# A perceiver block on one core: the low parts of the next tile's query products for the last four heads on GpSimd instead of VectorE

## The reference

```python
q = layernorm(x) @ Wq;  k = ctx @ Wk;  v = ctx @ Wv        # split into 16 heads of 64
scores = einsum('bhsd,bhkd->bhsk', q, k) / 8
x = x + einsum('bhsk,bhkd->bhsd', softmax(scores), v).reshape(B, S, 1024) @ Wo + bo
x = x + self_attention(layernorm(x));  x = x + quantised_ffn(layernorm(x))
```

## Time and profile before

| | |
|---|---|
| median of the runs | 1576.76 us (1576.45 to 1576.85) |
| the profiled execution | 1575.99 us, span 1574.2 us |
| busy: TensorE, its weight loads | 1536.0 us (98%), 1282.0 us (81%) |
| busy: VectorE, ScalarE, GpSimd | 1058.1 us (67%), 737.9 us (47%), 371.2 us (24%) |
| low parts on VectorE, line 1086 | 62 of 1749 ns, 107.2 us |
| low parts on GpSimd, line 1314 | 2 of 3499 ns |
| cross attention by tiles | from about 188 to 1005 us of the span |
| granted TensorE clock | 0.996 |

### The profile page before, as it was taken

The page is one execution under the profiler, slowest core; times in us unless marked ns, Lnnn a source line. Parts: engine busy times, 40 slices in busy tenths (PEclk is TensorE's granted clock), DMA queues, the critical chain, the costliest instruction groups (busy, mean ns, idle before and its releaser), DMA issues.

```text
span 1574.2 us, 35899 instructions
## 1 busy us (share of the span) xinstructions
PE 1536.0 (98%) x13706; PEld 1282.0 (81%) x13714; DVE 1058.1 (67%) x2295; ACT 737.9 (47%) x1596; POOL 371.2 (24%) x225
## 2 busy tenths in 40 slices
PE   7999999999999999999999999999999999998989
PEld 5778788888998899989988898888878888786544
DVE  7666677677667766676677667647555654556788
ACT  5444655555545554555455554433222232224755
POOL 1000235343444344444434343500000000000000
PEclk9999999999999999999999999999999999999999
DMA  6899873341434233332333133250220311225022
GB/s 234 318 365 360 316 252 128 138 149 49 140 132 144 61 122 138 138 92 91 138 138 128 63 139 130 82 201 22 78 98 29 115 49 42 101 63 155 0 107 107
DMA packets 90237, 210.72 MB, mean 134 GB/s; under 512 B 16992, under 2 KB 45856, under 8 KB 87328
## 3 DMA queue, kind: packets, MB, share of 16 engines
q1 hardware_dynamic: 90144, 209.39, 37.6%
HBM read 137.54 MB, written 68.94 MB: 131 GB/s over the span
## 4 chain that ended last, share of the span: by engine, by line
PE 75%; issue 12%; DVE 9%; ACT 4%; DMA 0%; DVEq 0%; SPq 0%; ACTq 0%; POOLq 0%; POOL 0%
PE psum_o L688 13%; PE psum_s L665 7%; PE psum_q L665 7%; PE psum_o L1482 6%; PE psum_q L1522 6%; PE psum_q L1482 6%; PE psum_t L1554 6%; PE psum_o L553 5%; PE psum_o L703 5%; DVE qk L1086 3%; PE psum_t L676 3%; PE psum_t L634 2%; PE psum_s L1509 1%; PE psum_t L585 1%; PE psum_q L585 1%
## 5 line engine op out<-in xcount | busy, mean ns | idle before, releaser
L688 PE MATMUL psum_o<-pT,c_nat 128*128 128x512 f32 x1152 | 307.4, 403 | 3.4 <-issue 2.4
L688 PEld LDWEIGHTS psum_o<-pT,c_nat 128*128 128x128 f32 x1152 | 202.7, 188 | 38.8 <-DVE pT L951 3.6
L1298 POOL TENSOR_TENSOR c_nat<-c_raw,constants 128x768 fp32r<-128x768 f32 x64 | 93.9, 1467 | 560.7 <-PE psum_o L688 445.4
L1152 DVE TENSOR_SCALAR oT<-psum_o,c_last 128x512 f32<-128x512 f32 x192 | 143.4, 747 | 65.8 <-PE psum_o L688 65.7
L665 PE MATMUL psum_s<-cT,qk 128*128 128x256 f32 (+1 forms) x1152 | 167.8, 288 | 2.2 <-DVE cT L951 0.3
L665 PEld LDWEIGHTS psum_s<-cT,qk 128*128 128x128 f32 x1152 | 151.1, 190 | 11.2 <-DVE cT L951 5.1
L665 PE MATMUL psum_q<-cT,qk 128*128 128x256 f32 (+1 forms) x1152 | 152.9, 284 | 1.0 <-DVE qk L1086 1.0
L878 ACT ACTIVATE probs<-psum_s,nmax 128x257 f32<-128x257 f32 x128 | 61.1, 477 | 197.4 <-DVE nmax L1167 197.4
L665 PEld LDWEIGHTS psum_q<-cT,qk 128*128 128x128 f32 x1152 | 143.4, 190 | 4.0 <-issue 2.6
L951 DVE TENSOR_TENSOR pT<-psum_t,pT 128x512 fp32r<-128x512 f32 x128 | 87.7, 686 | 71.0 <-ACT pT L769 71.0
L1283 POOL TENSOR_TENSOR c_raw<-c_raw,last_row 128x768 f32<-128x768 f32 x64 | 120.2, 1878 | 29.4 <-DMA last_row<-in_ctx_dram 19.0
(11 more groups left out here) (292 smaller groups left out, 3092.1 us busy)
## 6 DMA issues: line engine op xcount, KB each, us to landing
qk_by_tile<-staged SPq DMA_DIRECT2D x32, 1536.0 KB, 10.2
raw<-qk_by_tile SPq DMA_DIRECT2D x16, 3072.0 KB, 12.3
c_raw<-in_ctx_dram SPq DMA_DIRECT2D x64, 384.0 KB, 3.2
last_row<-in_ctx_dram SPq DMA_DIRECT2D x64, 192.0 KB, 4.0
out_dram<-x_out SPq DMA_DIRECT2D x32, 256.0 KB, 2.0
x_res<-in_x_dram SPq DMA_DIRECT2D x16, 256.0 KB, 2.7
x_in<-out_dram SPq DMA_DIRECT2D x4, 1024.0 KB, 8.3
x_all<-out_dram SPq DMA_DIRECT2D x1, 4096.0 KB, 13.2
```

Source lines behind the costliest of these rows:

```text
L688: i = pe.matmul(ps[:], c_nat[(b - 1) % 2][:, part, k, m * P:(m + 1) * P], pT[:, moving, k, :], start=(k, part, moving) == (0, 0, 0), stop= ...
L1152: nc.vector.tensor_scalar(oT[:, m, :, (b - 1) % 4, :], ps[:].rearrange("p (s q) -> p s q", q=SQ), c_last[:, (b - 1) % 2, m:m + 1], None, A ...
```

## The change

Low part 3 of the next tile (heads 12 to 15) is no longer made by VectorE, for tiles 1 to 15. GpSimd makes it: in tile 0 behind its last subtraction of the last key, in tiles 1 to 14 behind split and subtraction of batch 3, in a new function `pool_qk_low_last`. It signals a semaphore of its own, `s_qlo3`. `s_qlo` now rises by three a tile from tile 1 on, and the counts that TensorE and SyncE wait for follow. GpSimd's wait for all low parts at the start of tile 1 is gone; SyncE's load of the next `raw` waits for both semaphores.

```diff
--- before.py
+++ after.py
@@ -440,6 +440,7 @@
         s_qraw = sem("qk_tile_loaded")
         s_qhi = sem("qk_high_ready")
         s_qlo = sem("qk_low_ready")
+        s_qlo3 = sem("qk_low_of_last_heads_ready")
         s_sub = sem("ctx_less_last_key")
         s_zero = sem("last_scores_zeroed")
         s_chi = sem("ctx_high_ready")
@@ -654,7 +655,12 @@
             if section == "first" and rg == 0 and b < 2:
                 pe.wait_ge(s_zero, b + 1)
             if b == 0:
-                pe.wait_ge(s_qlo, 4 * t + (rg + 1))
+                if section == "first":
+                    pe.wait_ge(s_qlo, rg + 1)
+                elif rg < 3:
+                    pe.wait_ge(s_qlo, 3 * t + (rg + 2))
+                else:
+                    pe.wait_ge(s_qlo3, t)
             ps, done = empty(pe, U1(("S", b, rg), t, section))
 
             keys = SKP if section == "first" or (b, rg) == (0, 3) else 2 * P
@@ -1235,7 +1241,6 @@
                     ctxT(b, 2)
                     dve_attended(dve, t, b, 1, section)
                     dve_qk_low(dve, t + 1, 2, section)
-                    dve_qk_low(dve, t + 1, 3, section)
                     dve_attended(dve, t, b, 2, section)
                     continue
                 if qk_next:
@@ -1307,6 +1311,14 @@
             pool.wait_ge(s_xres, 16 * t)
             nc.gpsimd.tensor_tensor(x_res[:], x_res[:], bo_all[:], ALU.add).then_inc(s_xb, 1)
 
+        def pool_qk_low_last(pool, t, section):
+
+            full(pool, U1(("S", 3, 3), t - 1, section))
+            pool.wait_ge(s_qhi, 4 * t + 4)
+            part = [qk[:, i, 3, :, :, :].rearrange("p c b (h q) -> p h (c b) q", h=4) for i in range(2)]
+            nc.gpsimd.tensor_tensor(part[1], raw[:, :, 3, :].rearrange("p h (a q) -> p h a q", q=SQ),
+                                    part[0].bitcast(F32), ALU.subtract).then_inc(s_qlo3, 1)
+
         def pool_qk_low(pool, t, rg):
 
             pool.wait_ge(s_qhi, 4 * t + (rg + 1))
@@ -1327,11 +1339,11 @@
                 pool_less_last(pool, 0, b)
                 pool_split(pool, 0, b, "first")
             pool_less_last(pool, 0, 4)
+            pool_qk_low_last(pool, 1, "first")
 
         def pool_cross_tile(pool, t, section):
             for b in range(4):
                 if section == "second" and b == 0:
-                    pool.wait_ge(s_qlo, 4 * t + 4)
                     pool_less_last(pool, t, b + 1)
                     pool_split(pool, t, b, section)
                     continue
@@ -1340,6 +1352,8 @@
                     pool_less_last(pool, t, b + 1)
                 if b == 1:
                     pool_bias(pool, t)
+                if b == 3 and section != "last":
+                    pool_qk_low_last(pool, t + 1, section)
             if section == "last":
                 pool_first_self_norm(pool)
 
@@ -1428,7 +1442,8 @@
                     sp.wait_ge(s_nat, 4 * t + (b + 1))
                     load_ctx(sp, 4 * t, b + 2)
                 if b == 0:
-                    sp.wait_ge(s_qlo, 4 * t + 4)
+                    sp.wait_ge(s_qlo, 3 * t + 4)
+                    sp.wait_ge(s_qlo3, t)
                     if more:
                         load_qk(sp, t, 1)
                     else:
```

## The result

| | before | the change |
|---|---|---|
| median of the runs | 1576.61 us | 1593.68 us (1593.49 to 1595.75, four runs) |
| ratio to before | | 1.0112 (95%: 1.0094 to 1.0129) |
| the profiled execution, and its span | 1575.99, 1574.2 us | 1595.75, 1594.0 us |

The account below looks back on a forecast made before the run. TensorE, 394 matmuls a tile end to end, was taken as the bound, delayed only by late results. Loop +18.3 us and first border -0.8 made +17.5 on 1576.76, so 1594.3 us; range 1577 to 1600 us.

Parts of the forecast that it names:

- The place and the start: Border between two tiles, end of batch 3: GpSimd starts 0.08 us behind ScalarE's last high part, 0.35 us ahead of VectorE.
- The exclusion: In the loop's borders, GpSimd's subtraction shuts out VectorE's for heads 8 to 11, which then lasts about 4.7 us.
- two meetings ahead of the loop: At 195.32 and 21.15, VectorE operations waited on GpSimd subtractions: 1.62 us instead of 0.345, and 2.70 instead of 2.288.
- Rivals 1 and 3: At the borders, 1: no exclusion, 1570.5 us, chance 0.12; 3: exclusion not whole, engines take turns, about 1585 us, chance 0.06.
- The end of the hold: In the loop's borders, VectorE is shut out until 0.17 us before GpSimd's recorded end, so until 490.91.
- the estimate of 4 us more in all: In the loop's borders, with the skill page's 115 ns, VectorE's wait would be 0.28 us longer each.
- The sum for a border: Loop borders: VectorE's queue moves 1.31 us later, TensorE's wait grows from 0.33 to 1.64 us; 14 x 1.31 = +18.3 us.
- the upper bound of the gain, 4.6 us: In the loop, removing TensorE's 14 waits of 0.33 us for the context's low part gives back 4.6 us at most.
- The first border: After tile 0, VectorE goes first and GpSimd ends at about 237.2; gain 0.8 us, between 0 and 1.7.
- rival 4: At the loop's borders, the longer stall halves the clock for 3.4 us, up to 14 x 1.7 more: 1618 us; chance 0.03.
- Rival 2: In the loop VectorE gets in first and GpSimd's split follows late, a new TensorE wait of 0.5 us; 1578.8 us, chance 0.08.

Follow-up runs that it names:

- border0_as_before: The changed kernel with tile 0 as before: VectorE makes both last low parts and GpSimd waits for them at the start of tile 1; 1595.24 us.
- change_again: The changed kernel as it is, measured again beside other kernels on the same chip; 1594.85 us.
- vector_first: Against the changed kernel, GpSimd starts its subtraction only when VectorE has ended the one for heads 8 to 11; 1578.49 us.
- two_halves: Against the changed kernel, GpSimd's subtraction is cut into two instructions of 768 columns each, back to back; 1570.09 us.

## Why the prediction was right, step by step

**The place and the start.** Forecast: GpSimd starts 0.08 us behind ScalarE, 0.35 ahead of VectorE. Measured: 0.08 and 0.36.

**The exclusion.** This was the step on which the sign hung, drawn from two meetings ahead of the loop. VectorE's subtraction was to last about 4.7 us; it lasts 4.75 to 4.87 in the 14 borders, and GpSimd's 3.51 on average. That it is these two instructions and nothing else about GpSimd's work is shown by leaving out either (51.00 us both times), by turning their order round (15 us back) and by cutting the one in half (24 us back). Rivals 1 and 3 fall with that. One reading behind the step was too broad: in the loop of before, VectorE operations on on-chip memory alone do meet GpSimd's, namely the reciprocals of one column. They keep their length, at most 0.168 us for any of the 256; one stands here beside the GpSimd instruction in whose time it runs:

```profile
496.08 0.15 DVE L1171 RECIPROCAL rden<-den 128x1 f32<-128x1 f32 x1
...
495.01 1.85 POOL L1283 TENSOR_TENSOR c_raw<-c_raw,last_row 128x768 f32<-128x768 f32 x1
```

**The end of the hold.** I took 0.17 us ahead of GpSimd's recorded end, the rows show 0.14. The Trainium skill, page "SBUF — State Buffer", section "SBUF: two separate sides", says that of a VectorE instruction with two inputs in on-chip memory and a GpSimd instruction that reads it, the one that starts first has the port pair that they share for its whole length, while the other is blocked fully. By that rule, the trace agrees: 4.76 us for 1.75 of work. The 115 ns behind the winner's end that the same page of the Trainium skill gives were measured on a DMA that waited for GpSimd to write its descriptors behind a VectorE copy. I took them over to two compute instructions; here the waiting one goes on 0.14 us before the other's recorded end, and the estimate of 4 us more in all did not come.

**The sum for a border.** Forecast +1.31 us, measured 52.74 - 51.38 = +1.36. The mechanism is as written: wait of the weight loads from 0.33 to 1.68 us (forecast 1.64), no second one. The loop is 14 x 1.36 = 19.0 us instead of 18.3. Of the 0.05 us between the two sums 0.03 are VectorE's subtraction, 4.76 us where the forecast's times make it 4.73. That a recorded wait costs a little more than its length (0.33 us cost 0.38, 1.68 cost 1.74, against 51.00) hardly enters the difference, but the upper bound of the gain, 4.6 us, should have been 5.3.

**The first border.** Forecast: TensorE's scores for heads 12 to 15 wait until 237.3, the next product starts at 238.5, a gain of 0.8 us. GpSimd was to take about 4.8 us there; it takes 4.70, and the scores start at 237.22. In that place the mechanism is as written, and the gain is 0.94 us in the records of the two kernels above. But I stopped the sum there, and the second meeting in tile 1 takes the gain back: the term of -0.8 us is nothing in the end (44.76 us against 44.81). In the profiled execution of the change tile 1 went another way, by something that I had given 0.03, and for the loop: the granted clock stood at half (the 1.2 GHz level) from 237.66 to 241.07 us of its span, so the nine matmuls took 2.01 us instead of 1.34:

```profile
232.47 4.70 POOL L1319 TENSOR_TENSOR qk<-raw,qk 128x1536 fp32r<-128x1536 f32 x1 [7.28 <-ACT qk L817]
...
237.22 2.01 PE L671 MATMUL psum_q<-cT,qk 128*128 128x258 f32 x9 [1.99 <-POOL qk L1319]
...
237.00:240.60 3.60, 3.38 (x13) 3.09 (x14) 1.54 (x6) 2.50 (x8) 3.52 (x4) 0.58 0.00 0
```

(The last row is the windows view; 0.58 is the mean granted clock of that stretch.) The nine matmuls and what follows cost it some 1.5 us; with that VectorE no longer met the addition of the bias (TensorE's wait there is 0.23 us), and tile 1 with its border ended 0.5 us longer than in before. This execution was also the longest of the four, 1595.75 us against 1593.49 to 1593.73 with mean clocks of 0.995 and 0.996 to 0.997. In the loop rival 4 did not happen: 14 stalls of 1.68 us, and a granted clock of 1.00 throughout. In the first border it comes and goes: border0_as_before had it in its profile as well, change_again had not.

**Why the total is still 17.1.** The loop costs 19.0 us, not 18.3, and the first border gives nothing back, not 0.8. The profiled executions bear that sum out: the spans of the change and of change_again are 19.8 and 18.9 us above that of before, where the forecast was 17.5 for just this difference. The medians give 17.1 in the first comparison and 18.0 (1594.85 less 1576.86) in the second. Part of the gap to the profiles is that the profiled execution of before was 0.6 and 0.9 us below the two medians of before; the rest is within the spread between executions (1575.02 to 1578.17 for before alone in the second). So the mechanism and the loop were right, but that 17.1 lies 0.4 us from my 17.5 is chance: the two terms each missed by 0.7 to 0.8 us in the same direction, and a sum of 19 would have been the right one.

**Rival 2,** an exclusion with VectorE first, was made by vector_first. I had priced it at 1578.8 us; it takes 1578.49, 1.7 us above before as measured beside it. Who comes first does decide between +17 and +2 us, by 0.36 us of lead. That the price fits so closely is in part luck: its new wait is 0.83 us and not 0.5, the loop costs 14 x 0.25 = 3.4 us and not 2.8, and the gain of 0.8 in the first border isn't there.

## What to carry to other kernels

Before work is moved from VectorE to GpSimd, list what VectorE does in the time of the moved instruction. Here a VectorE instruction on two whole tensors in on-chip memory waited for the end of a GpSimd subtraction or addition of such tensors, each time that the two met with GpSimd first; one that read a PSUM bank never did in these profiles (the 192 low parts of the context took at most 0.43 us each, in before as in the change). So work that was taken from a queue can make that queue later. If two such instructions must meet, let the one that TensorE waits for go first, by a semaphore if need be, or cut the GpSimd instruction into pieces shorter than what can be borne; then look at what GpSimd's own lateness delays, and put the step that is due first at the head of its queue. A third of a microsecond of lead made the difference between a loss of 0.1% and one of 1.1%, and the order of GpSimd's steps that between a loss of 0.1% and a gain of 0.3%. And a gain in one place can move an engine into a new meeting further on: follow it to the next common point before it is put into a sum.

## What the runs showed of the hardware

- A stall of some 2 us in the first border was followed by a granted clock of half for 3.4 us in some executions and not in others with the same code there: 1.99 us in the change but not in change_again, 2.44 in border0_as_before but not in before. Stalls of 2.13 to 2.30 us in four other kernels were followed by none, nor were the 14 of 1.68 us, one in 52.7 us, in any of the three profiles that have them (the granted clock is 1.00 from 286 to 1012 us).
- The turn can change after one instruction: in two_halves VectorE came in between two GpSimd instructions that stood back to back in the queue, where with one long GpSimd instruction it waited 3.01 us for its end. But it is not a strict turn. In before, at the end of cross attention, a GpSimd operation with per-partition scalars took 6.30 us instead of 2.09; it was next from about 999.25 us, and two VectorE subtractions that began then, back to back, both went ahead of it:

```profile
L1003 POOL TENSOR_SCALAR x_in<-x_in,group_ln x4: 2073/2092/6300, 997.2 to 1007.6; 128x512 f32<-128x512 f32 x4
...
999.25 4.52 DVE L1858 TENSOR_TENSOR w2q_low<-w2q_raw,w2q_high 128x2048 fp32r<-128x2048 f32 x2 [0.15 <-ACT w2q_high L1675]
```

- VectorE's operations that read a PSUM bank ran beside GpSimd at full speed (0.43 and 0.74 us), even with a second operand in on-chip memory, and so did the reciprocals of one column (0.15 us). The scalings of probabilities did not beside GpSimd's two-tensor instructions (1.62 us instead of 0.345 for one), but did 0.6 us into a GpSimd operation with per-partition scalars. No run was made to find out why.
